# A routed feed-forward layer on one core: second-layer weight halves side by side, rows written a block later

## The reference

```python
buf = zeros(E, C, D).at[idx, pos_safe].set(x, mode='drop')
hmid = relu(einsum('ecd,edf->ecf', buf, w1) + b1)     # 256 -> 1024
ybuf = einsum('ecf,efd->ecd', hmid, w2) + b2          # 1024 -> 256
y = ybuf[idx, pos_g] * (prb * kept)
y = nan_to_num(y, nan=0.0, posinf=10000.0, neginf=-10000.0)
x = x + y
```

## Time and profile before

| what | value |
|---|---|
| median of 3 runs | 1419.08 us (1413.65 to 1420.54) |
| the profiled execution's own time | 1418.93 us |
| its span, first to last instruction | 1417.1 us |
| mean granted TensorE clock | 0.939 |
| TensorE busy | 1220.0 us (86%) |
| TensorE's weight loads | 1068.4 us (75%) |
| VectorE busy | 1005.7 us (71%) |
| ScalarE busy | 954.8 us (67%) |
| GpSimd busy | 1006.8 us (71%) |

### The profile page before, as it was taken

How to read it: one execution, slowest core, us unless ns; L and a number is a source line. 1 busy time by engine, 2 the same in 40 slices (tenths; PEclk the granted TensorE clock), 3 DMA queues, 4 the chain that set the end, 5 groups by cost and what they waited for, 6 DMA issues and landing times.

```text
span 1417.1 us, 26819 instructions
## 1 busy us (share of the span) xinstructions
PE 1220.0 (86%) x7869; PEld 1068.4 (75%) x7870; DVE 1005.7 (71%) x2164; ACT 954.8 (67%) x2127; POOL 1006.8 (71%) x913
## 2 busy tenths in 40 slices
PE   2487678888899146999999999999999999999995
PEld 0244344555565036999999999999999999999995
DVE  7999997998799894756657555755755575556754
ACT  3789897886566364767667666766666776666673
POOL 6888778876588205767778767777776787678874
PEclk9977766999999587999999999999999999999998
DMA  9789996555667003533434333433423352233333
GB/s 326 224 277 284 275 219 168 74 77 111 183 211 266 2 10 95 111 45 47 110 45 84 75 46 46 109 49 49 111 46 44 46 116 46 45 48 52 53 54 40
DMA packets 131810, 153.02 MB, mean 108 GB/s; under 512 B 17218, under 2 KB 118658, under 8 KB 131606
## 3 DMA queue, kind: packets, MB, share of 16 engines
q0 software_dynamic: 51328, 64.07, 28.8%
q1 hardware_dynamic: 58758, 66.60, 14.6%
q10 hardware_dynamic: 21648, 21.49, 4.5%
HBM read 98.30 MB, written 53.81 MB: 107 GB/s over the span
## 4 chain that ended last, share of the span: by engine, by line
PE 56%; issue 2%; ACT 2%; POOL 1%; DMA 1%; DVE 0%; ACTq 0%; POOLq 0%
PE f_ps_y L1713 28%; PE f_ps_h L1701 26%; PE f_ps_x L1691 2%; ACT y_all L1651 1%; DMA sg<-stat_rows,idx_now 1%; ACT h_hi L1640 0%; ACT h_all L1641 0%; POOL xg L1446 0%; POOL sg L1452 0%; ACT f_xn L1625 0%; POOL out L1585 0%; DVE clean_end L1828 0%; DVE clean_end L1827 0%; ACT f_xn L1602 0%; DVE y_sum L1808 0%
## 5 line engine op out<-in xcount | busy, mean ns | idle before, releaser
L1640 ACT ACTIVATE h_hi<-f_ps_h,c_b 128x384 fp32r<-128x384 f32 (+1 forms) x416 | 236.4, 568 | 267.3 <-PE f_ps_h L1701 267.3
L1751 DVE TENSOR_TENSOR h_lo<-h_all,h_hi 128x768 fp32r<-128x768 f32 (+1 forms) x208 | 184.2, 885 | 255.8 <-ACT h_all L1641 255.1
L1713 PE MATMUL f_ps_y<-w_hi,h_hi 128*128 128x256 f32 x1136 | 325.4, 286 | 0.0
L1713 PE MATMUL f_ps_y<-w_hi,h_lo 128*128 128x256 f32 x1136 | 320.5, 282 | 0.0
L1713 PE MATMUL f_ps_y<-w_lo,h_hi 128*128 128x256 f32 x1136 | 319.2, 281 | 0.0
L1563 POOL DMA_INDIRECT out<-clean,put_now x156 | 257.1, 1648 | 56.7 <-issue 47.0
L1701 PE MATMUL f_ps_h<-x_hi,w_hi 128*128 128x384 f32 (+1 forms) x832 | 270.9, 326 | 9.4 <-issue 3.4
L1446 POOL DMA_INDIRECT xg<-out,idx_now x156 | 186.8, 1197 | 127.2 <-issue 119.6
L1701 PE MATMUL f_ps_h<-x_lo,w_hi 128*128 128x384 f32 (+1 forms) x832 | 268.0, 322 | 0.0
L1701 PE MATMUL f_ps_h<-x_hi,w_lo 128*128 128x384 f32 (+1 forms) x832 | 268.0, 322 | 0.0
L1641 ACT ACTIVATE h_all<-f_ps_h,c_b 128x384 f32<-128x384 f32 (+1 forms) x416 | 237.6, 571 | 0.0
(11 more groups left out here) (241 smaller groups left out, 2270.3 us busy)
## 6 DMA issues: line engine op xcount, KB each, us to landing
shared<-out SPq DMA_DIRECT2D x40, 512.0 KB, 4.2
w_raw<-in_w SPq DMA_DIRECT2D x16, 1024.0 KB, 5.2
xin<-in_x SPq DMA_DIRECT2D x24, 512.0 KB, 7.9
out<-xin ACTq DMA_DIRECT2D x24, 512.0 KB, 5.4
shared<-in_x SPq DMA_DIRECT2D x16, 512.0 KB, 5.3
out<-shared ACTq DMA_DIRECT2D x16, 512.0 KB, 5.0
dst_row<-in_dst SPq DMA_DIRECT2D x20, 256.0 KB, 4.9
xg<-out,idx_now POOLq DMA_INDIRECT x156
```

Source lines behind the costliest of these rows:

```text
L1640: nc.scalar.activation(h_hi[:, f, :n * P], ps_h[:, f % SLOTS, :n * P], ACT.Relu, bias=b1[:, e, f:f + 1])
L1713: ins = nc.tensor.matmul(ps_y[:, i], x[:, f, i * P:(i + 1) * P], weights[s][:, w], start=i != 1 and f == 0 and n == 0, stop=f == KF - 1 an ...
L1751: tt(h_lo[:, pair, :n * P], h_all[j % 2][:, :, :n * P], h_hi[:, pair, :n * P].bitcast(F32), ALU.subtract).then_inc(h_lo_ready, 1)
```

## The change

**Second layer.** The high and low half of each 256-column slice of the second weights lie side by side, and one product of 512 columns writes the high part's contribution of both into a whole bank per tile; the third product, of the low hidden part, adds 256 columns to the bank's second half. `ps_y` takes three banks, `ps_h` three instead of four. VectorE adds the two halves in two instructions.

**Rows a block later.** ScalarE does the eight relu pairs without a break, then normalises; `turn` stands after j == 1. The scaling goes to VectorE, and the rows of earlier blocks are handled in steps behind the splits j of the current block: the sum for block b - 2 and its predicated copy, the scaling of b - 1, its infinities. GpSimd writes the rows of block b - 3 after the gathers in its step, with one group of writes more at the start. Gathers are issued only for the tiles that a block has; SP counts them and tells ScalarE. All eight high weight parts are ScalarE's, all low parts VectorE's. GpSimd and SP loop per expert, for which routing makes a small table more.

**The ends of the stage.** In the first block the low parts come before the clearing of buffers. The last block's second layer goes tile by tile, and VectorE does each tile's sums, scaling and cleaning.

**Edge block.** The own rows of chunk 19 move behind the direction passes of group 10, their store behind the loop, and two prefetches move ahead of SP's wait for stores.

```diff
@@ edge_and_node_block, SP
+            next_receivers(STEPS - 1)
+            next_embedding(STEPS)
             for a in range(2):
                 sp.wait_ge(x1_out[(NC - 1) % RING][a], 16 * ((NC - 1) // RING + 1))
             sp.sem_inc(stored, 1)
-            next_receivers(STEPS - 1)
-            for g in range(STEPS, EG):
+            next_receivers(STEPS)
+            for g in range(STEPS + 1, EG):
@@ edge_and_node_block, ScalarE
             for g in range(1, STEPS):
                 add_own_rows(2 * g)
                 radial_hidden(g + 1)
-                if g + 1 == STEPS:
-                    add_own_rows(2 * g + 1)
-                    store_rows(NC - 1, 1)
                 next_rows(g + 1)
                 rows_by_direction(g + 1, (0, 1))
                 take_agg(g - 1)
                 if g + 1 < STEPS:
                     add_own_rows(2 * g + 1)
                 rows_by_direction(g + 1, (2, 3))
+                if g + 1 == STEPS:
+                    add_own_rows(2 * g + 1)
                 take_upd(g - 1)
+            store_rows(NC - 1, 1)
...
@@ expert_block, GpSimd
+            def step(b, tiles):
+                pool.wait_ge(xn_ready, b)
+                pool.wait_ge(prob_next_ready, b)
+                pool.sem_inc(spare_pool, 1)
+                gather(b, tiles)
+                add_rows(b - 3)
...
+            for e in range(NEXP):
+                start, wide, end = bounds(pool, e)
+                if e == 0:
+                    with pool.Fori(2, end) as b:
+                        step(b, BT)
+                else:
+                    with pool.Fori(start, wide) as b:
+                        step(b, 2)
+                    with pool.Fori(wide, end) as b:
+                        step(b, BT)
+            last = last_bound(pool)
+            add_rows(last - 2)
+            add_rows(last - 1)
...
@@ expert_block, ScalarE
             def step(e, b, n, split=None):
+                if split is not None:
+                    for c in range(AHEAD):
+                        weights.split_high(nc, act, e + 1, split, c)
                 for f in range(KF):
                     relu(e, b, f, n)
-                    if f == 1:
-                        scale_rows(b - 1)
-                    if f == 3:
-                        act.wait_ge(turned, b + 1)
-                        act.sem_inc(spare_act, 1)
-                        normalise(b + 1)
...
+                act.wait_ge(turned, b + 1)
+                act.sem_inc(spare_act, 1)
+                normalise(b + 1)
...
                 take_high(b + 1)
@@ expert_block, TensorE
+            def down(s, j, i):
+                for f in (2 * j, 2 * j + 1):
+                    w = w_down[s][f // HALF]
+                    nc.tensor.matmul(ps_y[:, i], h_hi[:, f, i * P:(i + 1) * P], w[:, f % HALF],
+                                     start=f == 0, stop=False)
+                    ins = nc.tensor.matmul(ps_y[:, i, 1], h_lo[:, f, i * P:(i + 1) * P], w[:, f % HALF, 0],
+                                           start=False, stop=f == KF - 1)
                 return ins
...
+            def step(e, b, tiles):
+                first_layer(e, b, tiles)
                 for j in range(KJ):
-                    ins = down(b, e % 2, j, tiles)
-                    if j == 0:
+                    hidden_ready(b, j)
+                    for i in range(tiles):
+                        ins = down(e % 2, j, i)
+                    if j == 1:
                         turn(b + 1)
                 ins.then_inc(y_ready, 1)
@@ expert_block, VectorE
+            def rows_of_earlier_blocks(b, j):
+                if j == 0:
+                    add_infinities(b - 2)
+                if j == 1:
+                    keep_finite(b - 2)
+                if j == 2:
+                    scale_rows(b - 1)
+                    next_prob(b)
+                if j == 3:
+                    find_infinite(b - 1)
 
             def step(e, b, n, split=None):
                 for j in range(KJ):
                     split_hidden(b, j, n)
-                    if j == 0:
-                        next_prob(b)
-                        find_infinite(b - 1)
+                    rows_of_earlier_blocks(b, j)
...
                 take_low(b + 1)
-                add_infinities(b - 1)
-                keep_finite(b - 1)
...
                 v.wait_ge(y_ready, b + 1)
-                tt(y_sum[:, :n], ps_y[:, :n], b2[:, bass.ds(e, 1)].broadcast_to([P, n, D]),
-                   ALU.add).then_inc(y_sum_ready, 1)
+                v.sem_inc(spare_dve, 1)
+                tt(y_sum[:, :n], ps_y[:, :n, 1], b2[:, bass.ds(e, 1)].broadcast_to([P, n, D]),
+                   ALU.add).then_inc(y_step, 1)
+                v.wait_ge(y_step, 3 * b + 3)
+                v.sem_inc(spare_dve, 1)
+                tt(y_sum[:, :n], ps_y[:, :n, 0], y_sum[:, :n], ALU.add).then_inc(y_sum_ready, 1)
```

More of the change, by code:

```diff
@@ L1316, in _ @@
             chain.link(ins)
-            chain.link(tt(place[:], place[:], chosen[:], ALU.mult))
+            chain.mark(nc.vector.tensor_tensor_scan(wide_upto[:], ones_row[:, :NEXP], wide[:], 0.0, ALU.mult, ALU.add))
+            chain.mark(nc.vector.tensor_copy(wide_blocks[:, 0], wide[:1]))
+            chain.mark(tt(place[:], place[:], chosen[:], ALU.mult))
+            chain.wait(1)
+            chain.mark(stt(out=wide_blocks[:, 1], in0=wide_upto[:1], scalar=narrow[:1, 0:1], in1=wide[:1],
+                           op0=ALU.add, op1=ALU.subtract))
+            chain.wait(1)
             chain.link(red(packed[:], place[:], AX.X, ALU.add))
@@ L1542, in _ @@
             sp.wait_ge(gathers.stats_first, 16 * FIRST)
-            for e in range(1, NEXP):
-                sp.wait_ge(hi_ready, CUTS + BY_ACT * (e - 1))
-                sp.wait_ge(lo_ready, CUTS * e)
-                weights.load(sp, e)
+            for e in range(NEXP):
+                if e + 1 < NEXP:
+                    sp.wait_ge(hi_ready, CUTS * (e + 1))
+                    sp.wait_ge(lo_ready, CUTS * (e + 1))
+                    weights.load(sp, e + 1)
+                start, wide, end = bounds(sp, e)
+                if e == 0:
+                    with sp.Fori(1, end) as b:
+                        sp.wait_ge(gathered, 64 * b)
+                        sp.sem_inc(spare_sp, 1)
+                        sp.wait_ge(gathered_third, 32 * b)
+                        sp.sem_inc(rows_in, 1)
+                else:
+                    with sp.Fori(start, wide) as b:
+                        sp.wait_ge(gathered, 64 * b)
+                        sp.sem_inc(rows_in, 1)
+                    trips = sp.value_load(wide_blocks[0:1, 0, bass.ds(e, 1)], min_val=1, max_val=NB)
+                    thirds = sp.value_load(wide_blocks[0:1, 1, bass.ds(e, 1)], min_val=LEAST, max_val=NB)
+                    with sp.Fori(0, trips) as b:
+                        sp.wait_ge(gathered, 64 * b + 64 * wide)
+                        sp.sem_inc(spare_sp, 1)
+                        sp.wait_ge(gathered_third, 32 * b + 32 * thirds)
+                        sp.sem_inc(rows_in, 1)
             for n in range(2):
@@ L1604, in normalise_first @@
                 ins.then_inc(xn_ready, 1)
+                indices(1)
             def take_high_first():
@@ L1679, in _ @@
                     step(e, b, 2)
-                step(e, wide, BT, 1 - e % 2 if e + 1 < NEXP else None)
-                with act.Fori(wide + 1, end) as b:
-                    step(e, b, BT)
-            scale_rows_end(end - 1)
+                if e + 1 < NEXP:
+                    step(e, wide, BT, 1 - e % 2)
+                    with act.Fori(wide + 1, end) as b:
+                        step(e, b, BT)
+                else:
+                    last = last_bound(act)
+                    with act.Fori(wide, last) as b:
+                        step(e, b, BT)
+                    for f in range(KF):
+                        relu(e, last, f, BT)
         @block.tensor
```

254 lines of the change are left out of this document (135 added, 119 removed).

## The result

The changed kernel takes 1448.9 us, the median of 4 runs (1443.87 to 1452.75), against 1419.16 before: a ratio of 1.0226, 95% interval 1.0202 to 1.0249, 29.7 us slower. It is the fastest of the four; the two slowest show a lower mean granted clock, 0.927 and 0.926 against 0.936, and the other 4.7 of the 29.7 us no trace shows.

A forecast was written before the change was run, and what follows sets the result against it. TensorE's work was taken to bound the expert stage, plus whatever holds it in narrow blocks. Terms -12.5 + 7.7 - 1.1 + 0.5 + 1.5 - 5.2 = -9.1 took 1418.93 to 1409.8, given as 1410 us, range 1400 to 1422.

The forecast's parts named there:

- What bounds the kernel: Expert stage: TensorE's work counts, 17.64 us a wide block without a gap; only narrow blocks have gaps.
- Products: Second layer: 512-column products save 11 ns in each of 1136 triples, 12.5 us less (bounds 0 and 15.4).
- Rival A: Second layer: a 512-column product costs as two of 256, so nothing is saved; 1422 us, chance 0.13.
- Waits that go in narrow blocks: Moving ScalarE's scaling to VectorE frees the first layer; narrow blocks take 12.05 us, 10.7 us less together.
- Waits that come: Narrow blocks: normalising ends late, and writes after the predicated copy delay the last block's gathers; 18.4 us more.
- rival B: Expert stage: the clock falls in the new waits; two of five would give +9.4 us, 1419; chance 0.13.
- 3.5 us of slack: Wide blocks: gathered rows land 6 us into the next block, against 9.5 needed, so no wait.
- Wide blocks behind wide ones: Next rows asked for at 12.5 us into a wide block; added VectorE work hidden, three first-layer buffers cost nothing.
- Start, routing, end: First block's start 1.1 us less, small VectorE operations in routing 0.5 more, last writes 1.5 more (1.3 to 5.6).
- Edge block: Own-row passes moved behind the next direction passes remove TensorE's 4.84 us wait and its half clock: 5.2 us less.
- the case that the clock falls anyway: Edge block: if the clock falls despite the moved passes, only 3.7 us are gained.
- Rival C: Writes hold up the next gathers in every wide block: 38 blocks at 1 us, 1448 us; chance 0.07.

The follow-up runs named there:

- experiment 6: The kernel of experiment 3 with its 512-column products cut into two of 256 columns again, on the same weight layout: 1407.30 us, ratio 0.9927.
- experiment 3: The changed kernel with VectorE's sum of infinities and predicated copy moved back to the end of the block after: 1398.67 us, ratio 0.9877 to the kernel before.
- experiment 4: The changed kernel with two of the three writes of every block but the last left out: 1396.15 us in one execution.
- experiment 1: The kernel before with the edge-block part of the change alone, including SP's two prefetches: 1414.17 us, ratio 0.9976.

## Why the prediction was wrong

The forecast was 1410, range 1400 to 1422; measured were 1448.9. Step by step:

- **What bounds the kernel** held: in wide blocks TensorE works without a gap, before and, but for two of them, after.
- **Products**, 12.5 forecast: the wide one takes 233 ns, beyond the 227 to 230 named and nearer to the gate's 230 than to the line through the earlier trace rows. A wide block is 0.22 us shorter, 9.2 ns a triple where 11 were taken, and 8.6 us came by experiment 6. Right in kind, a third of it did not come. Rival A, which gives the wide products nothing, is refuted by that experiment. The Trainium skill ("TensorE: Matmul & The Clock Gate", Back-to-back issue gap) gives columns at 2.4 GHz plus 2.5 ns for a product taken by itself, an estimated 216 ns for 512 columns and 109 for 256. This stream is slower: 512 columns take 233 ns here and 256 take 118.
- **Waits that go in narrow blocks**, 10.7 forecast: they did not go. The first narrow block of a run takes 12.7 us without a wait, not 12.05, since VectorE starts it with two additions of y and table reads, the first split ends at 971.97, 4.3 us in, and ScalarE's fifth pair needs it. Even in experiment 3 the 13 blocks are only 2.5 us shorter than before, products included. I had named ScalarE's scaling as the only thing that held the first layer; and of the 3.98 us that I gave it in expert 6, 1.48 were another wait, for normalised rows ahead of the transposes at 1299.24.
- **Waits that come**, the failed step: "some 3.3 us in the last of each run of two or more", five times, 16.2. The chain named was the right one, copy, GpSimd's start, writes, gathers, landing, normalising; three of its terms were too small. In expert 4 the copy ended 6.9 us in, not 6.0, the three writes took 6.05, not 5.7, and the six gathers 10.0, not 8.0, so that the transposes came at 27.1 instead of 23.9. The block they sit in had begun at 12.7, and they were wanted 8.7 into it, against 8.43 forecast. The waits in the last narrow blocks of experts 2, 4, 5 and 7 were 5.7 to 6.9, not 3.3; in expert 6 the middle block waited, 2.87 where 0.6 was forecast, and the last only 0.52. Then two things were left out: the clock, which I held apart as rival B with a chance of 0.13 (0.50 behind six waits, some 10 us by estimate), and the two first wide blocks after a single narrow one, 2.8 each, where I gave every wide block 3.5 us of slack. That slack was worked out for wide behind wide; behind a narrow one the block before is 4.7 shorter. The Trainium skill ("TensorE: Matmul & The Clock Gate", Why this matters for your kernels) warns against idle gaps of TensorE between bursts, since they bring the half clock back. This trace agrees behind six of its seven waits.
- **Wide blocks behind wide ones**: right, transposes 12.54 into the block against 12.5. The block lasts 17.40, as 17.64 less 24 x 0.011 would have it; the 17.1 to 17.2 named as a sign do not follow from the prediction's own terms.
- **Start, routing, end**: the first block -1.2 against -1.1 (in experiment 4, with the same order, 14.75, so -0.5); the edge block's lead of 7.4 at its last aggregation (354.67 to 347.24) is 6.9 at the first expert block. That is the 0.5 forecast for routing, but not shown: this stretch takes 190.0 to 190.4 in the four executions with the old routing and 190.1 to 190.6 in the five with the new. The end is +2.4 against +1.5, in the stated bounds. GpSimd's writes at the end of the changed kernel:

```profile
1414.63 1.69 POOL L1607 DMA_INDIRECT out<-clean,put_now  x1 [11.84 <-DVE clean L1841]
...
1425.74 1.55 POOL L1607 DMA_INDIRECT out<-clean,put_now  x1 [5.36 <-DVE clean L1841]
...
1435.12 1.55 POOL L1607 DMA_INDIRECT out<-clean_end,put_end  x1 [0.30 <-issue]
```

 Two rounds of waits for the copy (11.84 and 5.36), as forecast; the sixth write starts 28.9 after the last block, forecast 27.4.
- **Edge block**, 5.2 forecast: the order of the steps was right, TensorE in the changed kernel:

```profile
215.76 6.66 PE L646 MATMUL ps_agg<-same,msg 128*128 128x512 f32 x16
223.65 2.05 PE L654 MATMUL ps_agg<-lin,agg 128*128 128x128 f32 x16 [1.22 <-ACT agg L575]
...
231.42 7.34 PE L646 MATMUL ps_agg<-same,msg 128*128 128x512 f32 x16 [2.38 <-ACT rows L580]
```

 The transformation starts at 223.65, forecast 224.9, at full speed (2.05), and aggregation waits for ScalarE's copies of the update, forecast 233.5, found 231.42. But the half clock did not go, it came later: this aggregation took 7.34, where it takes 4.61 at full clock. Busy time, columns as in the earlier trace rows, first in the kernel before, right behind that row, then in the changed one:

```profile
238.70:244.60 5.90, 5.90 (x11) 3.29 (x11) 5.90 (x11) 5.07 (x11) 4.99 (x4) 0.50 0.32 88
```

```profile
230.30:237.00 6.70, 5.58 (x10) 3.29 (x11) 6.62 (x19) 5.87 (x12) 5.81 (x6) 0.50 1.00 248
```

 The 10.2 us of the earlier trace rows were not the whole stretch before, and another stretch followed after. The runs give 3.4, near the 3.7 that the prediction has for the case that the clock falls anyway. The time at half clock differs between executions (experiment 1), and one execution was no measure of it.
- **Slips in the sums**, none of which decides: two products of 256 columns less 226.7 leave 13.7 ns, not 13.5; five waits of 3.3 are 16.5, not 16.2; 27.4 - 26.1 is 1.3, not 1.5.

So two terms decided: 10.7 us of waits that did not go, and some 43 us that came, 32.9 of waits and some 10 of clock, where 18.4 were forecast. Rival C had the mechanism too, writes ahead of gathers. It looked for it in all 38 wide blocks, at a price of 38 us, so that its 1448 is near the measured time by luck: it came in 7 places at some 6 us each, the clock's share in, five of them narrow blocks.

## What to carry to other kernels

A queue that runs in order has two kinds of work with two deadlines; when a change moves the time at which the less urgent kind is ready, as the clean rows here, ask what it holds up while the queue waits for it. Check the slack at the shortest blocks and at the change from short to long, where it is smallest, and give each term of a long chain its spread, since a wait that is a difference of two long sums takes all of their error. And part a change that loses: here one copy's place cost 50 us and hid a version of 1398.

## What the runs showed that I had not expected

- Three buffers for the first layer instead of four, in the old order, cost 106 us (1417.4 to 1523.1), over ten times what the freed bank brings: 7% for a buffer. By the chain the fourth had covered ScalarE's 1.7 us of indices and normalising between two pairs.
- The last wide block of an expert took 18.27 us before, 0.64 more than the others; 0.48 of it is a pause ahead of the next block's first product, for which the chain shows no cause. It is gone in the changed kernel (17.40) and back in experiment 6 (18.26) with its three products per triple. What it is was not tried.
